# The last pair's token rows moved to the experts and back in pieces of three, sorted by TensorE

## The chip, the cores and the metric

The kernel runs on one core of one Trainium2 chip. The time is device microseconds of one execution. The core has five engines that each run a program of their own and meet through semaphores: PE (TensorE, matrix products), DVE (VectorE), ACT (ScalarE), POOL (GpSimd) and SP (SyncE, which here only issues DMAs).

## What is computed

One layer of a vision transformer on 16 images, 1024 tokens each, 64 channels: patches are embedded, a linear attention with a residual follows, and then a mixture of 16 experts of which every token uses its two best:

```python
logits = einsum('bsd,de->bse', x, gate_w) + gate_b
top_probs, top_idx = top_k(softmax(logits), 2)
top_probs = top_probs / sum(top_probs)
hidden = silu(einsum(x, w1[e])) * einsum(x, w2[e])      # per expert, 64 -> 128
out = h + sum over the token's two experts of top_probs[e] * (hidden @ w3[e])
```

The reference works out all 16 experts for each token. The kernel works out the two that count.

## The kernel before

**Pairs.** The images go through in 8 pairs, m = 0 to 7. A pair has 2048 tokens, which lie on the 128 partitions as 16 columns j. Each token has two expert places r = 0, 1.

**Sorting by expert.** DVE and PE find, for each token and each of its two experts, a row of a scratch tensor in DRAM in which the rows of an expert lie together, each expert padded to whole tiles of 128 rows (`place`). POOL sends the rows there: `scatter(m, j)` (L497) issues, for one column, two indirect DMAs of 128 rows of 512 B (the row of z in two parts, `z_parts`). So a pair has 32 scatters. When they have landed, SP loads the rows back in groups g of four tiles (`load_rows`, L364); a pair has 12 groups, all pairs 96, and g = 84 to 95 are those of pair 7.

**The experts, group by group.** `turn(g)` (PE, L1153) transposes the rows, ACT copies them to SBUF (`rowsT`, L608). `project_in(g)` (PE, L1169) first reads the experts of its four tiles into registers (L1162) and then multiplies with those experts' w1 and w2, in two halves, each as w_hi and w_lo. ACT takes a tanh of each half (`activate`, L618), DVE multiplies (`multiply`, L970 and L972: silu as 0.5 x (1 + tanh(x/2)) times the second product). `turn_hidden` (PE, L1179), `copy_hidT` (ACT, L626), `project_out` (PE, L1186), `copy_y` (ACT, L631) follow, and SP stores y to a second scratch tensor (L373).

**Back to the tokens.** `gather(m, j)` (POOL, L514) issues two indirect DMAs per column that read the token's two result rows of 256 B. For each quarter q of the columns, `weigh` (ACT, L643) multiplies the first by its gate and adds the mean, `sum_up` (DVE, L981, L985) adds the second times its gate and then h, and SP stores the result (L380). For pair 6 the gathered rows lie in the tiles hx and kexp, for the others in `sums`.

**What sets the order.** Every engine runs the same loop over steps s, each with its own list of what belongs to a step, and executes strictly in that order. Group g's `project_in` stands in step s = g + 23. Pair m's attention begins at step BEGUN[m]. The tables SCATTER and GATHER say at which step POOL starts pair m's scatters and gathers, SUMS at which step ACT and DVE weigh and sum quarter q. POOL has 8 x 32 scatters and 8 x 32 gathers, 512 DMAs; for pairs 6 and 7 it does: scatters of pair 7, gathers of pair 5, of pair 6, of pair 7. PE's step is project_in(g), turn_hidden(g - 1), attention, turn(g + 2), project_out(g - 2). ACT's is rowsT of g + 1, copy_y(g - 3), attention, activate(g), copy_hidT(g - 1), weigh. DVE's is attention, multiply(g), attention, sum_up.

Of the kernel before, what the change touches and what calls it, by code (L numbers as in the profile page):

```python
# [18 lines left out]
E = 64  # L19
# [8 lines left out]

GROUP = 4
GROUPS = 12  # L30
TILES = GROUP * GROUPS
assert TILES * P >= 2 * 2 * TOKENS + (EXPERTS - 1) * (P - 1)
SLOTS = TILES * P
# [10 lines left out]
    qturn mixed attend added squares2 ssq2 normed2 zturn zparts logits pick rank odds count base ends owner""")  # L44
# [3 lines left out]
             rank=14, odds=15, count=14, base=14.5, ends=14.5, owner=15)  # L48
# [3 lines left out]
             rank=16, odds=15.5, count=16.5, base=17, ends=17.5, owner=18)  # L52
# [57 lines left out]
def vit_kernel(nc, x, tok_w, tok_b, pos, wk, bk, wq, bq, wv, bv, wr, br, gate_w, gate_b, w1, w2, w3, out):  # L110
    xi_dram = nc.dram_tensor("xi_scratch", (2, 2, TOKENS, E), F32, kind="Internal").ap()
    rows_dram = [nc.dram_tensor(f"rows_scratch{n}", (SLOTS, 2 * E), F32, kind="Internal").ap() for n in range(3)]
    y_dram = [nc.dram_tensor(f"y_scratch{n}", (SLOTS, E), F32, kind="Internal").ap() for n in range(3)]
    with ExitStack() as ctx:
# [14 lines left out]
        before_f = sb("before_f", [P, P])  # L129
        before_b = sb("before_b", [P, P], BF16)  # L130
# [21 lines left out]
        br_in = sb("br_in", [P, E])  # L152
# [68 lines left out]
        tiles_all = sb("tiles_all", [EXPERTS, P])  # L221
# [18 lines left out]
        hidT = [hidT_all[:, n] for n in range(2)]  # L240

# [7 lines left out]
        def rows_of(place):  # L249
# [5 lines left out]
        zeros = tanh  # L255

# [16 lines left out]
            odds_sum_ready gate_ready gates_ready rank_ps_ready tiles_ready tiles_spread base_ps_ready ends_ready  # L273
            past_ready owner_ps_ready owner_ready ranked place_summed place_ready
# [6 lines left out]
        scattered = [sem(f"scattered{n}") for n in range(3)]  # L281
        rows_in = [sem(f"rows_in{n}") for n in range(3)]
# [6 lines left out]
        WEIGHTS = 7 + 6 + 2 + 2 + 10 + 2 + 1 + 2 + 3  # L289
# [33 lines left out]
        def part_of(m, n):  # L323
# [4 lines left out]
            return slice(t0, t1), src[:, 0:(t1 - t0) * 2 * MIXW].rearrange("p (t b e) -> p t b e", b=2, e=MIXW)  # L328

# [5 lines left out]
        def _(sp):  # L335
# [896 lines left out]
```

## Time and profile before

| | |
|---|---|
| median of 3 runs | 793.08 us (792.98 to 795.68) |
| profiled execution, its span | 791.9 us |
| PE busy | 578.2 us, 73% |
| POOL busy | 518.2 us, 65% |
| DVE busy | 441.7 us, 56% |
| ACT busy | 347.6 us, 44% |

The profile is of one execution with a span of 791.9 us, 1.2 us under the median of the timed runs. Busy shares are over the whole span; they do not say which engine is waited for at its end. Times in rows are microseconds from the start of the span, "[32.02 <-DMA ...]" is the idle time of that engine just before the row and what ended it, "issue" is idle time in which the engine waited for nothing that the profile shows. PE's ends are modelled, so its times are read from start to start.

### The profile page before, as it was taken

The page shows a single profiled execution, that of the slowest core. Times are in us where ns is not written, and L with a number is a line of the kernel's source. Part 1 is how long each engine was busy: PE and PEld are TensorE (multiplying, and loading weights), DVE is VectorE, ACT ScalarE, POOL GpSimd, SP SyncE. Part 2 cuts the span into 40 slices and gives each one's busy share as a digit, 9 for nine tenths or more (in the row PEclk, how much of TensorE's full clock was granted, in tenths as well). Part 3 has the DMA queues.
Part 4 walks back from the last instruction along what each step waited for, and adds up shares of the span by engine and source line. Part 5 has one row for each costly group of instructions (what it writes and reads, how often), then busy time and mean ns, then how long its engine had stood idle before and what let it go on. Part 6 is the DMA issues. An engine that isn't in the chain of part 4 may idle for free.

```text
span 791.9 us, 14201 instructions
## 1 busy us (share of the span) xinstructions
PE 578.2 (73%) x3856; PEld 476.0 (60%) x3856; DVE 441.7 (56%) x1237; ACT 347.6 (44%) x753; POOL 518.2 (65%) x540
## 2 busy tenths in 40 slices
PE   5967796787799989998899889998958702883000
PEld 3455545574588678867786678687958702873000
DVE  5664755556447686676667567756765601454111
ACT  2124122152456476647564566446626701674111
POOL 2052246576771777777777777777777777777774
PEclk9976796798999999999999999979979965996555
DMA  2499022333553375528542744374345414544111
GB/s 78 101 229 396 28 71 83 97 97 90 148 170 89 72 188 142 144 53 208 136 124 69 190 130 121 76 175 109 112 117 128 114 51 127 135 100 98 40 40 31
DMA packets 168871, 93.20 MB, mean 118 GB/s; under 512 B 99680, under 2 KB 152928, under 8 KB 168800
## 3 DMA queue, kind: packets, MB, share of 16 engines
q1 hardware_dynamic: 151632, 66.71, 32.1%
q0 software_dynamic: 16384, 25.20, 11.6%
q8 instruction: 39, 0.64, 0.3%
q10 hardware_dynamic: 784, 0.39, 0.2%
q14 instruction: 32, 0.26, 0.1%
HBM read 45.06 MB, written 47.19 MB: 116 GB/s over the span
## 4 chain that ended last, share of the span: by engine, by line
POOL 33%; PE 29%; issue 15%; DVE 13%; DMA 7%; ACT 3%; POOLq 0%; ACTq 0%; DVEq 0%; SPq 0%
POOL rows_scratch L497 15%; POOL sums L514 14%; PE wide_ps L1030 5%; PE h_ps L1169 4%; PE y_ps L1186 3%; DMA hx<-xi_scratch 3%; DMA xi_scratch<-xi 2%; POOL hx L514 2%; POOL kexp L514 2%; PE turn_ps L1153 2%; PE wide_ps L1050 2%; PE wide_ps L1129 1%; PE hidT_ps L1179 1%; PE wide_ps L1036 1%; DVE twice_y L970 1%
## 5 line engine op out<-in xcount | busy, mean ns | idle before, releaser
L497 POOL DMA_INDIRECT rows_scratch<-z_parts,place x256 | 254.9, 996 | 128.4 <-issue 74.7
L514 POOL DMA_INDIRECT sums<-y_scratch,place x224 | 213.8, 955 | 82.7 <-issue 66.4
L1169 PE MATMUL h_ps<-w_hi,rowsT 128*128 x384 | 111.5, 320 | 40.9 <-DVE hid_all L972 33.8
L970 DVE SCALAR_TENSOR_TENSOR twice_y<-tanh,h_ps 128x256 f32<-128x256 f32 x192 | 79.8, 416 | 101.3 <-ACT tanh L618 85.3
L1169 PEld LDWEIGHTS h_ps<-w_hi,rowsT 128*128 128x128 f32 x384 | 74.6, 194 | 55.8 <-issue 54.5
L1186 PE MATMUL y_ps<-w_sb,hidT_all 128*128 x768 | 100.9, 276 | 1.1 <-ACT twice_y L631 1.1
L1169 PE MATMUL h_ps<-w_lo,rowsT 128*128 x384 | 101.0, 290 | 0.0
L1186 PEld LDWEIGHTS y_ps<-w_sb,hidT_all 128*128 128x128 f32 x768 | 97.4, 199 | 2.2 <-issue 2.2
L1153 PE MATMUL turn_ps<-ident,rows_all 128*128 128x128 f32 x384 | 60.8, 282 | 46.3 <-DMA rows_all<-rows_scratch 39.8
L618 ACT ACTIVATE tanh<-h_ps 128x256 f32<-128x256 f32 x192 | 69.8, 387 | 56.3 <-PE h_ps L1169 50.0
L972 DVE SCALAR_TENSOR_TENSOR hid_all<-twice_y,h_ps 128x256 f32<-128x256 f32 x192 | 80.8, 421 | 6.6
L1153 PEld LDWEIGHTS turn_ps<-ident,rows_all 128*128 128x128 f32 x384 | 45.7, 145 | 60.0 <-DMA rows_all<-rows_scratch 40.3
L608 ACT ACTIVATE rowsT<-turn_ps 128x512 fp32r<-128x512 f32 x96 | 57.1, 594 | 44.8 <-PE turn_ps L1153 44.8
L1169 PEld LDWEIGHTS h_ps<-w_lo,rowsT 128*128 128x128 f32 x384 | 75.5, 197 | 0.2
L631 ACT ACTIVATE twice_y<-y_ps 128x256 f32<-128x256 f32 x96 | 36.7, 382 | 63.9 <-DMA y_scratch<-twice_y 51.5
L1179 PE MATMUL hidT_ps<-ident,hid_all 128*128 128x128 f32 x384 | 60.4, 282 | 0.5 <-DVE hid_all L972 0.5
L626 ACT ACTIVATE hidT_all<-hidT_ps 128x512 f32<-128x512 f32 x96 | 57.9, 603 | 5.5 <-PE hidT_ps L1179 2.8
L1030 PE MATMUL wide_ps<-w_patch,x_cols 64*128 64x512 f32 x224 | 57.6, 645 | 3.1 <-DVE w_patch L693 3.1
L981 DVE SCALAR_TENSOR_TENSOR sums<-sums,gate 128x64 f32<-128x64 f32 x112 | 24.5, 280 | 58.3 <-ACT sums L643 56.7
L643 ACT ACTIVATE sums<-sums,mean_all,gate 128x64 f32<-128x64 f32 x112 | 39.9, 430 | 35.8 <-DMA sums<-y_scratch,place 35.8
L1179 PEld LDWEIGHTS hidT_ps<-ident,hid_all 128*128 128x128 f32 x384 | 46.0, 145 | 0.7 <-DVE hid_all L972 0.7
L1030 PEld LDWEIGHTS wide_ps<-w_patch,x_cols 64*128 64x128 f32 x224 | 21.8, 200 | 23.5 <-issue 18.9
(252 smaller groups left out, 910.3 us busy)
## 6 DMA issues: line engine op xcount, KB each, us to landing
rows_all<-rows_scratch SPq DMA_DIRECT2D x96, 256.0 KB
y_scratch<-twice_y SPq DMA_DIRECT2D x96, 128.0 KB
rows_scratch<-tanh SPq DMA_DIRECT2D x3, 3072.0 KB, 19.4
xi_scratch<-xi SPq DMA_DIRECT2D x16, 256.0 KB
rows_scratch<-z_parts,place POOLq DMA_INDIRECT x256
hx<-xi_scratch SPq DMA_DIRECT2D x14, 256.0 KB
sums<-y_scratch,place POOLq DMA_INDIRECT x224
out<-sums SPq DMA_DIRECT2D x56, 64.0 KB
```

The lines of the kernel that those rows point to most:

```text
L497: gp.indirect_dma_start(rows_dram[n], bass.IndirectOffsetOnAxis(ap=place[m % RING][:, r, j:j + 1], axis=0), z_parts[m % 2][:, j // 2, j % ...
L514: gp.indirect_dma_start(y_of[r][apart(m)][:, j // 2, j % 2, :], None, y_dram[m % 3], bass.IndirectOffsetOnAxis(ap=place[m % RING][:, r, j: ...
L608: sc.activation(rowsT[g % 2][:, :], turn_ps[:, :], ACT.Copy).then_inc(S["rowsT_ready"], 1)
L618: sc.activation(tanh[:, j, :], h_ps[:, :].rearrange("p (j n h) -> p j n h", j=GROUP, n=2)[:, j, 0, :], ACT.Tanh, scale=0.5).then_inc(S["ta ...
L626: sc.activation(hidT[g % 2][:, :], hidT_ps[:, :], ACT.Copy).then_inc(S["hidT_ready"], 1)
L970: ve.scalar_tensor_tensor(twice[:, j, :], tanh[:, j, :], 1.0, halves[:, j, 0, :], ALU.add, ALU.mult).then_inc(S["twice_done"], 1)
L972: ve.scalar_tensor_tensor(hid[g % 2][:, j, :], twice[:, j, :], 0.5, halves[:, j, 1, :], ALU.mult, ALU.mult).then_inc(S["hid_done"], 1)
L1030: te.matmul(wide_ps[:, b * 512:(b + 1) * 512], x_cols[second(m)][half, j, :], w_patch[half, j, :, :].rearrange("p t e -> p (t e)"), start= ...
L1153: mm = te.transpose(turn_ps[:, j * P:(j + 1) * P], rows[g % 3][:, j, :, :].rearrange("p n e -> p (n e)"), ident[:, :])
L1169: mm = te.matmul(h_ps[:, j * 256:(j + 1) * 256], rowsT[g % 2][:, j * P:(j + 1) * P], w[:, bass.ds(experts[g][j], 1), :, :].rearrange("d a ...
L1179: mm = te.transpose(hidT_ps[:, j * P:(j + 1) * P], hid[g % 2][:, j, :], ident[:, :])
L1186: mm = te.matmul(y_ps[:, j * E:(j + 1) * E], hidT[g % 2][:, j * P:(j + 1) * P], w3_sb[:, bass.ds(e, 1), :].rearrange("h a d -> h (a d)"), ...
```

## The change

Only pair 7 (`PIECED`) is treated in a new way; registers are read differently for all groups.

- **Pieces.** For each column of pair 7 the 256 rows to be sent are first sorted by expert inside the column and cut into pieces of three neighbouring rows, 96 pieces at most. A piece is sent with one index: 16 DMAs of 96 pieces of 1536 B (`scatter_pieces`) in place of 32 of 128 rows. The tiles of pair 7 hold 126 rows (42 pieces), and pair 7 has 13 groups, g = 84 to 96.
- **Sorting by matrix.** `find_routes` (DVE) makes for each column a 128x288 matrix with a one where a token goes to a slot, `move_rows` (PE) multiplies three 128x96 parts of it with the rows, `take_piece` (ACT) copies the result (96x384) to SBUF. These stand in steps 98 to 102.
- **Gathering pieces.** 16 DMAs of 96 pieces of 768 B (`gather_pieces`). The results are put back by PE: `sum_pieces` multiplies them with one-hot matrices that hold the gates, so that weighing and adding the two experts is one accumulation, and `sum_up_pieces` (DVE) adds h. ACT's weigh and DVE's four instructions of sum_up drop out for pair 7.
- **The gates.** `find_gates(j)` (DVE) makes the 128x288 matrix of gates for column j = s - 108 at the end of its step, `turn_gates` (PE) transposes its three parts at the end of PE's step, `take_gates` (ACT) copies them at the end of ACT's step. These stand in steps 108 to 123.
- **Counting.** For pair 7 the places are worked out from counts per column with a few more matrices, one step more in its plan. POOL makes the constants for this in `sort_consts` (27 instructions) at its start, ahead of splitting the expert weights.
- **Registers.** `load_owners(g + 1)` stands behind the matmuls of project_in(g), and the check of the four values against their bounds is left out.
- **Tables.** GATHER of pair 5 goes from step 104 to 102, of pair 7 from 122 to 123; SUMS of pair 5 from 115-118 to 112-115, of pair 6 from 121-122 to 119-122, of pair 7 from 123-126 to 124-127.

```diff
+PIECE = 3
+PIECES = (2 * P + EXPERTS * (PIECE - 1)) // PIECE
+TILE_PIECES = P // PIECE
+R = TILE_PIECES * PIECE
+PIECED = (7,)
...
+ROUTES = (None, None, None, None, None, None, None, 196)
+GATES = 108
-GATHER = (38, 51, 65, 78, 91, 104, 111, 122)
+GATHER = (38, 51, 65, 78, 91, 102, 111, 123)
...
+            def scatter_pieces(m, j):
+                if j == 0:
+                    wait(pool, "piece_at_ready", 1)
+                    scatter_place(m)
+                wait(pool, "piece_ready", j + 1)
+                gp.indirect_dma_start(pieces_dram[m % 3], bass.IndirectOffsetOnAxis(ap=piece_at[0:PIECES, j:j + 1], axis=0),
+                                      pieces[j][0:PIECES, :], None).then_inc(pieces_out, 16)
...
+            def gather_pieces(m, j):
+                q = j // (COLS // QUARTERS)
+                if j == 0:
+                    for n in range(2):
+                        wait_on(pool, y_stored[n], 16 * ((START[m + 1] + 1 - n) // 2))
...
+                gp.indirect_dma_start(y_pieces[j][0:PIECES, :], None, y_dram[m % 3].rearrange("(c i) e -> c (i e)", i=PIECE),
+                                      bass.IndirectOffsetOnAxis(ap=piece_from[0:PIECES, j:j + 1], axis=0)).then_inc(gathered[0][q], 16)
...
+            def take_gates(j):
+                wait(act, "gates_ps_ready", j + 1)
...
+                sc.activation(pieces[j][0:PIECES, :], piece_place(j)[0:PIECES, 0:PIECE * P], ACT.Copy).then_inc(S["gates_turned"], 1)
...
                 for m, q in sums_at(s):
-                    weigh(m, q)
+                    if m not in PIECED:
+                        weigh(m, q)
+                if 0 <= s - GATES < COLS:
+                    take_gates(s - GATES)
...
+            def find_routes(m, js):
+                for j in js:
...
+                    ve.tensor_scalar(route[i % ROUTE_RING][:, :, :], slot_id[:, :, :], slot[:, 0, j:j + 1], None,
+                                     ALU.is_equal).then_inc(S["route_begun"], 1)
+                for j in js:
...
+                    ve.scalar_tensor_tensor(route[i % ROUTE_RING][:, :, :], slot_id[:, :, :], slot[:, 1, j:j + 1],
+                                            route[i % ROUTE_RING][:, :, :].bitcast(F32), ALU.is_equal, ALU.add).then_inc(S["route_ready"], 1)
+            def find_gates(j):
...
+                wait(dve, "gates_ps_ready", j - 1)
+                wait(dve, "route_gated", 3 * j)
+                there, gated = gated_route[j % 2][:, :, :], gated_route[2][:, :, :]
+                ve.tensor_scalar(there, slot_id[:, :, :], slot[:, 0, j:j + 1], gate[n][0][:, j:j + 1], ALU.is_equal, ALU.mult).then_inc(S["route_gated"], 1)
+                ve.tensor_scalar(gated, slot_id[:, :, :], slot[:, 1, j:j + 1], gate[n][1][:, j:j + 1], ALU.is_equal, ALU.mult).then_inc(S["route_gated"], 1)
+                wait(dve, "route_gated", 3 * j + 2)
+                ve.tensor_tensor(there, there, gated, ALU.add).then_inc(S["route_gated"], 1)
...
                 for m, q in sums_at(s):
-                    sum_up(m, q)
+                    if m in PIECED:
+                        sum_up_pieces(m, q)
+                    else:
+                        sum_up(m, q)
+                if 0 <= s - GATES < COLS:
+                    find_gates(s - GATES)
...
+            def turn_gates(j):
+                wait(pe, "route_gated", 3 * j + 3)
+                wait(pe, "piece_ready", COLS)
+                wait(pe, "gates_turned", j - 1)
+                for n in range(PIECE):
+                    mm = te.transpose(piece_place(j)[0:PIECES, n * P:(n + 1) * P], gated_route[j % 2][:, n, :], ident[:, :])
+                mm.then_inc(S["gates_ps_ready"], 1)
+            def sum_pieces(m, q):
...
+                    for n in range(PIECE):
+                        mm = te.matmul(quarter_place(q)[:, i * E:(i + 1) * E], pieces[j][0:PIECES, n * P:(n + 1) * P],
+                                       y_pieces[j][0:PIECES, n * E:(n + 1) * E], start=(n == 0), stop=(n == PIECE - 1))
...
-                _, experts[g] = nc.values_load_multi_w_load_instructions(owner[m % 3][0:1, i * GROUP:(i + 1) * GROUP], engines=[te.engine],
-                                                                         min_val=0, max_val=EXPERTS - 1)
...
+                if g + 1 < GROUPS_ALL:
+                    load_owners(g + 1)
...
                 for m, k in steps_at(s):
                     attend(m, k + 0.75)
+                if 0 <= s - GATES < COLS:
+                    turn_gates(s - GATES)
+                for m, q in sums_at(s):
+                    if m in PIECED:
+                        sum_pieces(m, q)
```

On POOL, the scatters of pair 7 before, behind the gathers of pair 4 (`sums`, L514) and ahead of those of pair 5:

```order
L514 DMA sums<-y_scratch,place 128x64 x32
L497 DMA rows_scratch<-z_parts,place 6144x128 x32
L514 DMA sums<-y_scratch,place 128x64 x32
L514 DMA hx<-y_scratch,place 128x64
L514 DMA kexp<-y_scratch,place 128x64
```

And now, where the pieces lie in tiles that are free by then (w_patch, x_in, x_cols, squares):

```order
L691 DMA sums<-y_scratch,place 128x64 x32
L661 DMA rows_scratch<-w_patch,piece_at 3744x384 x10
L661 DMA rows_scratch<-x_in,piece_at 3744x384 x2
L661 DMA rows_scratch<-x_cols,piece_at 3744x384 x2
L661 DMA rows_scratch<-squares,piece_at 3744x384 x2
L691 DMA sums<-y_scratch,place 128x64 x32
L691 DMA hx<-y_scratch,place 128x64
L691 DMA kexp<-y_scratch,place 128x64
```

The 32 scatters are 16 DMAs of pieces; the 32 gathers at the end of POOL's program are 16 of L703 in the same way.

On PE, the end of a group's step and the start of the next, before, among the last groups of pair 7 (L1186 is project_out, L1162 the registers, L1169 project_in):

```order
L1186 ISA
L1186 MATMUL y_ps<-w_sb,hidT_all 128x64
L1162 TENSOR_LOAD owner
L1162 ISA x8
L1169 ISA
L1169 MATMUL h_ps<-w_hi,rowsT 128x256
```

And now (L1614 is project_out, L1548 turn_gates, L1593 project_in, L1577 load_owners, L1606 turn_hidden):

```order
L1614 ISA
L1614 MATMUL y_ps<-w_sb,hidT_all 128x64
L1548 MATMUL wide_ps<-ident,gated_route 96x128 x3
L1593 ISA
L1593 MATMUL h_ps<-w_hi,rowsT 126x256
```

The reading of the registers and the 8 rows of the check are gone from ahead of project_in; in their place stand, in steps 108 to 119, three transposes that wait for DVE.

On ACT, one step of the last groups now (L807 rowsT, L833 copy_y, L818 tanh, L827 copy_hidT, L860 weigh, L848 take_gates):

```order
L807 ACTIVATE rowsT<-turn_ps 128x504
L833 ACTIVATE twice_y<-y_ps 126x256
L818 ACTIVATE tanh<-h_ps 126x256 x2
L827 ACTIVATE hidT_all<-hidT_ps 128x504
L860 ACTIVATE sums<-sums,mean_all,gate_0 128x64 x4
L848 ACTIVATE w_patch<-wide_ps 96x384
L807 ACTIVATE rowsT<-turn_ps 128x504
```

Before, the rows of such a step were the same without L848: the copy of the gates now stands between a step's weigh and the next step's rowsT, copy_y and tanh.

## Rows read from the trace of the kernel before

**Rows 1.** The page: the chain that ended last, by line.

```profile
POOL rows_scratch L497 15%; POOL sums L514 14%; PE wide_ps L1030 5%; PE h_ps L1169 4%; PE y_ps L1186 3%; DMA hx<-xi_scratch 3%; DMA xi_scratch<-xi 2%; POOL hx L514 2%; POOL kexp L514 2%; PE turn_ps L1153 2%; PE wide_ps L1050 2%; PE wide_ps L1129 1%; PE hidT_ps L1179 1%; PE wide_ps L1036 1%; DVE twice_y L970 1%
```

**Rows 2.** POOL from 252 us on: gathers (busy us, mean ns | idle before), timeline.

```profile
L514 POOL DMA_INDIRECT sums<-y_scratch,place x224 | 213.8, 955 | 82.7 <-issue 66.4 <-PE turn_ps L1153 15.9 <-DMA y_scratch<-twice_y 0.3
...
252.40 0.98 POOL L514 DMA_INDIRECT sums<-y_scratch,place  x1 [14.73 <-PE turn_ps L1153]
```

**Rows 3.** POOL's timeline (start us, us) at the ends of its last stages.

```profile
622.77 1.03 POOL L497 DMA_INDIRECT rows_scratch<-z_parts,place  x1 [0.30 <-issue]
...
662.01 0.96 POOL L497 DMA_INDIRECT rows_scratch<-z_parts,place  x1 [0.30 <-issue]
...
743.74 0.94 POOL L514 DMA_INDIRECT sums<-y_scratch,place  x1 [0.30 <-issue]
...
782.82 0.94 POOL L514 DMA_INDIRECT sums<-y_scratch,place  x1 [0.30 <-issue]
```

**Rows 4.** Timeline of the end.

```profile
785.18 1.43 ACT L643 ACTIVATE sums<-sums,mean_all,gate 128x64 f32<-128x64 f32 x4 [8.60 <-DMA sums<-y_scratch,place]
...
787.55 0.42 DVE L985 TENSOR_TENSOR sums<-sums,h 128x256 f32<-128x256 f32 x1
```

**Rows 5.** Where pair 7's rows arrive: SP's timeline, and PE's.

```profile
664.27 0.37 SPq L364 DMA_DIRECT2D rows_all<-rows_scratch  x1
...
667.17 1.12 PE L1153 MATMUL turn_ps<-ident,rows_all 128*128 128x128 f32 x4 [32.02 <-DMA rows_all<-rows_scratch]
```

**Rows 6.** PE's timeline in the last groups: first matmul of project_in.

```profile
678.80 0.38 PE L1169 MATMUL h_ps<-w_hi,rowsT 128*128 x1
...
700.26 0.38 PE L1169 MATMUL h_ps<-w_hi,rowsT 128*128 x1 [0.63 <-DVE hid_all L972]
```

**Rows 7.** Weight loads of w_hi from 675 to 720 us, by line.

```profile
L1169 PEld LDWEIGHTS h_ps<-w_hi,rowsT 128*128 128x128 f32 x48 | 9.0, 187 | 8.3 <-issue 8.3
```

**Rows 8.** ACT's and DVE's timelines in a late step with weigh and sum_up.

```profile
704.55 0.87 ACT L618 ACTIVATE tanh<-h_ps 128x256 f32<-128x256 f32 x2 [0.91 <-PE h_ps L1169]
...
707.30 0.58 ACT L608 ACTIVATE rowsT<-turn_ps 128x512 fp32r<-128x512 f32 x1
...
708.18 0.90 ACT L618 ACTIVATE tanh<-h_ps 128x256 f32<-128x256 f32 x2
...
708.68 0.41 DVE L970 SCALAR_TENSOR_TENSOR twice_y<-tanh,h_ps 128x256 f32<-128x256 f32 x1
709.13 0.42 DVE L972 SCALAR_TENSOR_TENSOR hid_all<-twice_y,h_ps 128x256 f32<-128x256 f32 x1
709.46 0.41 DVE L970 SCALAR_TENSOR_TENSOR twice_y<-tanh,h_ps 128x256 f32<-128x256 f32 x1
```

**Rows 9.** DVE, by line: a TENSOR_SCALAR of 128x512.

```profile
L722 DVE TENSOR_SCALAR qv_bias<-ones 128x512 fp32r<-128x512 f32 x1 | 0.4, 361 | 0.0
```

**Rows 10.** Timeline: a TENSOR_SCALAR that starts during a DMA of POOL.

```profile
357.96 0.94 POOL L514 DMA_INDIRECT sums<-y_scratch,place  x1 [0.31 <-issue]
...
358.40 0.54 DVE L934 TENSOR_SCALAR tiles_all<-ones,tiles 16x128 f32<-16x128 f32 x1
```

**Rows 11.** Windows: busy us of each engine, granted clock, DMA share, GB/s.

```profile
57.00:60.00 3.00, 1.88 (x8) 1.48 (x8) 1.01 (x2) 0.29 (x1) 3.00 (x2) 0.66 1.03 382
471.00:474.00 3.00, 1.58 (x12) 1.44 (x12) 2.93 (x8) 2.21 (x8) 2.39 (x3) 1.00 0.72 199
675.00:720.00 45.00, 37.17 (x297) 35.21 (x297) 24.22 (x68) 31.64 (x77) 34.03 (x37) 0.99 0.49 117
```

**Rows 12.** The last y: timeline; and DMA issues with us to landing.

```profile
720.64 1.97 PE L1186 MATMUL y_ps<-w_sb,hidT_all 128*128 x8 [0.67 <-ACT twice_y L631]
...
723.05 0.37 SPq L373 DMA_DIRECT2D y_scratch<-twice_y  x1
...
out<-base SPq DMA_DIRECT2D x8, 64.0 KB, 1.7
```

**Rows 13.** POOL from 0 to 60 us, by line.

```profile
L479 POOL CAST w_hi<-sums 128x1024 fp32r<-128x1024 f32 x4 | 4.1, 1037 | 43.6 <-DMA w_sb<-in_L_ffn_w 43.6
```

More of the change, by code:

```diff
@@ L27 @@
 COLS = 2 * BLOCKS
-GROUP = 4
[L30 to L33, printed above, removed]
+PIECE = 3
[3 more added lines that the diff above has]
+PIECED = (7,)
+GROUP = 4
+GROUPS = tuple(13 if m in PIECED else 12 for m in range(PAIRS))
+START = tuple(sum(GROUPS[:m]) for m in range(PAIRS + 1))
+GROUPS_ALL = START[PAIRS]
+TILES = GROUP * max(GROUPS)
+assert GROUP * min(GROUPS) * P >= 2 * 2 * TOKENS + (EXPERTS - 1) * (P - 1)
+assert PIECES <= P and TILES >= (COLS * PIECES + EXPERTS * (TILE_PIECES - 1)) // TILE_PIECES
+SLOTS = TILES * R
+SPARE = -(-SLOTS // (PIECE * PIECES))
+DRAM_PIECES = (SPARE + COLS) * PIECES
+BOTH = 512
+assert PIECE * PIECES <= BOTH and SLOTS * BOTH < 2 ** 23 and (SPARE + COLS) * PIECE < 256
+ROUTE_RING = 3
 MIXW = E + 1
@@ L97, in apart, with nth, width, pair_of @@
     return int(m == APART)
+def nth(m):
+    return sum(n < m for n in PIECED)
+def width(m):
+    return R if m in PIECED else P
+def pair_of(g):
+    m = max(n for n in range(PAIRS) if START[n] <= g)
+    return m, g - START[m]
 def summed_there(m):
     return -1 if apart(m) else m - 2 if m == PAIRS - 1 else m - 1
-GROUPS_ALL = GROUPS * PAIRS
 HALVES = (slice(0, GROUP // 2), slice(GROUP // 2, GROUP))
@@ L240, in vit_kernel @@
         hidT = [hidT_all[:, n] for n in range(2)]
+        one = PIECE * 2 * E
+        flat = (w_patch[:, :, :, :].rearrange("p j t e -> p (j t e)"), x_in0[:, :, :].rearrange("p r f -> p (r f)"),
+                x_cols0[:, :, :].rearrange("p j c -> p (j c)"), squares[:, :])
+        pieces = [place[:, n * one:(n + 1) * one] for place, count in zip(flat, (10, 2, 2, 2)) for n in range(count)]
+        assert len(pieces) == COLS and one == PIECE * P
         x_in = (x_in0[:, :, :], twice_y[:, :].rearrange("p (r f) -> p r f", r=2))
@@ L304, in sums_at, with routes_at @@
                         yield m, q
+        def routes_at(half):
+            for m in PIECED:
+                for j in range(COLS):
+                    if ROUTES[m] + j // 2 == half:
+                        yield m, j
         def wait(eng, name, count):
@@ L328, in part_of, with wait_scattered, piece_place, quarter_place @@
             return slice(t0, t1), src[:, 0:(t1 - t0) * 2 * MIXW].rearrange("p (t b e) -> p t b e", b=2, e=MIXW)
+        def wait_scattered(eng, m):
+            if m in PIECED:
+                eng.wait_ge(pieces_out, 16 * COLS)
+            else:
+                eng.wait_ge(scattered[m % 3], 16 * 2 * COLS * sum(n % 3 == m % 3 and n not in PIECED for n in range(m + 1)))
+        def piece_place(j):
+            return wide_ps[:, j % 2 * 512:(j % 2 + 1) * 512]
+        def quarter_place(q):
+            return (turn_ps[:, 0:COLS * E // QUARTERS], hidT_ps[:, 0:COLS * E // QUARTERS],
+                    h_ps[:, 0:COLS * E // QUARTERS], h_ps[:, 512:512 + COLS * E // QUARTERS])[q]
         def x_half(m, b, par):
@@ L529, in gathers_at @@
                             yield m, j
+            sort_consts()
             split_experts()
@@ L534, in _ @@
                     wait(pool, "rowsT_ps_ready", min(s - LAG + 2, GROUPS_ALL))
+                for half in (2 * s - 1, 2 * s):
+                    for m, j in routes_at(half):
+                        scatter_pieces(m, j)
                 for m, j in scatters_at(s):
@@ L664, in _ @@
                     copy_hidT(g - 1)
+                for m, j in routes_at(2 * s - 1):
+                    take_piece(m, j)
                 for m, k in steps_at(s):
@@ L1111, in attend @@
+                if k == plan.base and m not in PIECED:
+                    wait(pe, "tiles_spread", m + 1)
+                    te.matmul(slots, tiles_all[0:EXPERTS, :], tiles_to_rows[:, :, :].rearrange("q j e -> q (j e)"), start=False, stop=True)
+                    te.matmul(side_ps[0:EXPERTS, 259:260], upto[:, :], tiles[:, :], start=True, stop=True).then_inc(S["base_ps_ready"], 1)
                 if k == plan.owner:
@@ L1200, in _ @@
                     attend(m, k)
+                for m, j in routes_at(2 * s - 1):
+                    move_rows(m, j)
                 if 0 <= g + 2 < GROUPS_ALL:
```

429 lines of the change are left out of this document (349 added, 80 removed).

## The prediction

> **What bounds the kernel now.** I read the page first. PE has the most busy time, but that is a share over the whole span; the chain that ended last is led by POOL's scatters (L497) and gathers (L514) [rows 1]. So I asked who POOL waits for. From 252.40 us on, its gathers wait for next to nothing: of 82.7 us idle in 224 gathers 66.4 is "issue", the 0.30 between two DMAs, and of the rest one wait of 14.73 ends exactly at 252.40 [rows 2]. Of the 512 DMAs 96, the scatters of pairs 0 to 2, lie before that. The other 416 are a conveyor whose last one starts at 782.82: 530.4 / 415 = 1.28 us each. The reader should see that the rate does not depend on bytes: a scatter writes 512 B per row and took 0.96 at 662.01, a gather reads 256 B and took 0.94 at 782.82 [rows 3].
>
> Then the last part of the conveyor [rows 3]: the scatters of pair 7 from 622.77 to 662.01, the gathers of pairs 5 and 6 up to 743.74, those of pair 7 to 782.82. Behind the last lie its landing, the weighing on ACT, the sum on DVE and the store to the end at 791.9 [rows 4].
>
> PE is the opposite case: it stands still for 32.02 us until pair 7's rows arrive at 667.17 [rows 5], works through the last groups at 3.58 us each (678.80 to 700.26 is six) [rows 6], and the last y goes to its store at 723.05, 20 us before POOL starts to gather from it [rows 3, 12]. This slack of 20 us is where the change puts work.
>
> **The change part by part.**
>
> *POOL.* 32 + 32 DMAs of pair 7 become 16 + 16. From 743.74 to 782.82 are 31 intervals of 1.26 us, so 32 x 1.26 = 40.2 us. The trace has no DMA of 96 pieces of 1536 or 768 B. Bounds: paid by bytes, 0.96 against 0.94 for twice as many adds 0.02 per doubling, up to 1 us in all, and if the longest DMA beside a busy DVE (1.03 at 622.77) became the rule, 3; fewer index rows (96 for 128) could gain as much. I take 1.26. Pair 7's last scatter then starts at 622.77 + 15 x 1.26 = 641.7, and POOL has done pairs 5 and 6 at 642.9 + 80.5 = 723.4.
>
> *Making the pieces* (find_routes, move_rows, take_piece, steps 98 to 102). For 16 columns DVE has 16 x (0.36 + 0.42) = 12.5 us more [rows 8, 9], in order with multiply. Some of it falls into DVE's idle time; I charge 10.5 (0 to 12.5). PE reaches the turn of group 84 at 635.15 now (667.17 less 32.02), so at some 645.7. The rows come when the last scatter has landed: the load was issued 2.26 after that scatter's start (662.01, 664.27) and PE got its rows 2.90 later. With 0.5 more for the larger scatter, an estimate, T0 = 641.7 + 2.8 + 2.9 = 647.3. The making is hidden by the stall; without that cover it would cost the 10.5.
>
> *Registers.* Before each group PE reads four owners and checks them, ahead of the weight load of w_hi, whose idle time is "issue": 8.3 us for 12 groups [rows 7]. That is what this edit can give, 0.7 a group. After 252.40 POOL hides it. Some 16 groups run ahead of it, 11 us at most; part of their time is a wait for loads, so I take 4 (0 to 11). Against it stand 27 POOL instructions of sort_consts. They lie in POOL's idle 43.6 us ahead of w_hi [rows 13], but read beside DVE's first work: no row shows them together, and I take 2 (0 to 5). Net gain at 252.40: 2 us (-5 to +11).
>
> *The gates* (find_gates, turn_gates, take_gates, steps 108 to 123). This decides. DVE makes column j's gates behind multiply(g), PE turns them at the end of the same step, ahead of project_in(g + 1), and ACT copies them at its step's end, ahead of the next tanh. So steps that overlapped become a ring: project_in, tanh, multiply, gates, turn, copy, tanh. Let gates be ready at W. From rows 8, a hand-over between engines is 0.11 (ACT's two tanh start at 708.18 and take 0.90 together, so the first ends some 0.39 in; DVE starts at 708.68).
> - Four turns took 1.12 at the low clock [rows 5], so three at full clock about 0.47; with two hand-overs the copy starts at W + 0.69.
> - rowsT and copy_y hold ACT 0.88 together (707.30 to 708.18), so 0.44 for a copy, and three copies stand ahead of tanh: W + 2.01. DVE's first multiply is at W + 2.51, and its four instructions follow by 0.45, 0.33, 0.45, 0.33: done at W + 4.07.
> - find_gates: a TENSOR_SCALAR of 128x512 took 0.36 [rows 9]; I take 0.35 twice for 128x288 with two pointers, and 0.46 for the sum of 288 columns (256 took 0.42 [rows 4]). Next gates at W + 5.23, with DVE's own hand-over **5.3 us a step** in place of 3.58.
>
> Bounds: 0.25 for each gives 5.1; 0.54 for each, the longest small one [rows 10], 5.7. PE's own work fits in: 37.17 us in 45 for 12 groups, 3.1 each [rows 11].
>
> In steps 112 to 115 and 119, weigh and sum_up of pairs 5 and 6 stand ahead of the gates. From tanh (704.55) to the DVE instruction behind sum_up (708.68) is 4.13, against 2.06 without: 7.4 us. Step 120 has no tanh: 0.69, two copies and hidT's (1.32), weigh to sum_up 2.37 and 0.42 [rows 4], gates 1.16, so 6.0; step 121 has one copy less, 5.5.
>
> Step 108 starts some 10 us after T0 (11.6 before, 667.17 to 678.80, after a long stall; 7.2 for two groups at 3.58), at 657.3. Seven steps of 5.3, five of 7.4 and 6.0 are 80.1: 737.4; step 121 ends at 742.9. The last copy_y is behind the copy of the gates: 0.69 + 0.44 + 0.39, 744.4. The store takes a hand-over, 0.37 and 1.7 [rows 12]: 746.6. POOL, ready at 723.4, waits there **23 us**. The stall moves from PE to POOL.
>
> A rule that speaks against the change: a TENSOR_SCALAR of 16x128 that started 0.44 us into a POOL DMA took 0.54 [rows 10], more than the 0.36 of one of four times as many columns [rows 9]. So some of the 28 TENSOR_SCALARs of the ring will be held by some 0.27 each; at one in four, 2 us, which stand in the range. The Trainium skill, "SBUF — State Buffer", section "Who interferes with whom", says more: DVE in a two-port mode, which tensor_scalar can enter, and GpSimd lock each other out for a whole instruction. By that sentence alone each would wait for the rest of the DMA that runs; the one row agrees that there is a hold, and does not show its full length.
>
> *The clock.* In three us with 1.88 us of PE work the granted clock fell to 0.66, in others with 1.58 it stayed at 1.00 [rows 11]; the ring has some 1.75 of 3 (3.1 in 5.3). At the low level the three turns take some 0.4 more, 14 x 0.4 = 6; more when PE's work, slowed to half, exceeds the ring. I take 2 (0 to 10).
>
> *The end.* 746.7 + 15 x 1.25 = 765.4, landing 2.36 [rows 3, 4]: 767.8. sum_pieces of the last quarter: 12 matmuls of fp32 in two passes, 24 records; eight of y_ps took 1.97 at the low clock [rows 12], so 3.0 to 5.9: 4. DVE's sum starts at 771.9, and as now 4.35 are left (787.55 to 791.9): 776.3.
>
> Sum: 776.3 - 2 + 2 = 776.3 of span. The profiled span of before is 791.9, 1.2 under the median 793.08; with that, **777.5 us**, 2% faster, where POOL alone would have given 5%.
>
> **The rivals.**
> - *POOL stays the bound.* If the ring were hidden, all 40.2 us come out: 791.9 - 40.2 - 2, plus 1.8 for PE's sum in place of weigh and sum_up, plus 1.2: 753. It needs y stored by 723.4, so 14 steps shorter by 1.7 us each. For it: 20 us of slack and no checks on PE. Against: each term of the ring has a row.
> - *A part of it.* A ring of 4.6 (copies that overlap more, a larger register part) gives 14 x 0.7 = 10 less: 767.
> - *The slower side: DVE locked out by POOL.* If a TENSOR_SCALAR waits for the whole DMA that runs, and the next DMA gets in between the two, each waits up to 0.95: 14 x 1.9 = 27, so 804. With the mean rest, 0.36 each (half of 0.95, in 0.95 of 1.26 us), 14 x 0.72 = 10: 787. From 1.4 us a step upward it is slower than before by over 0.5%. For it: 0.54 in rows 10. Against: it started 0.50 before that DMA's end and was held for about half of that. The section of the Trainium skill named above is the rule behind this case.
> - *No change:* 12 us more from clock, locks and a late PE at T0 together give 789.
>
> **How the numbers follow.** A measurement tells about 0.5%, 4 us, from no change: faster is under 789.1, slower over 797. Chances: my forecast (767 to 789) 0.62; POOL as the bound 0.18; between them 0.08; no change 0.06; slower 0.06. The range, which may leave out 2 in 10, goes from POOL's bound, 752, to 789; that of the likeliest case alone is 767 to 787.
>
> **What would show it.** Right: in the waits of POOL one of about 23 us at pair 7's first gather, for a y store; 480 DMAs; from 657 to 740 DVE, PE and ACT idle for each other in turn, project_in every 5.3 and 7.4 us; PE's stall at T0 under 5 us. Wrong: if POOL's idle is still 0.3 everywhere, POOL stayed the bound; if L1277 or L1278 has means over 0.6 us, DVE was locked out; if the DMAs of L661 and L703 are far from 0.95 us, the conveyor does not run by the DMA; if PE has no stall at T0, the pieces were made too late.

## The result and the profile after

The changed kernel takes 780.56 us (median of 4 runs, 778.07 to 784.67) where the kernel before takes 793.15 in the same comparison: a ratio of 0.984, 95% interval 0.981 to 0.987. The forecast was 777.5. The profiled execution has a span of 782.9 us, so it lies at the slow end of the four; before, it was 791.9. Two executions that count as slow, 798.52 us of the registers alone and 765.11 us of both edits again, stand in the medians and ranges below, but not in the ratios.

The waits of POOL behind 260 us (engine, line, released by: us in total, times, longest), POOL's two groups of piece DMAs, and POOL's timeline answer to [rows 2, 3]:

```profile
POOL sums L703 <- DVE base L1317: 24.6, 1, 24.6
```

```profile
L703 POOL DMA_INDIRECT sums<-y_scratch,piece_from x16 | 14.8, 925 | 29.2 <-DVE base L1317 24.6 <-issue 4.6
L661 POOL DMA_INDIRECT rows_scratch<-w_patch,piece_at x10 | 9.9, 992 | 3.0 <-issue 2.1 <-ACT w_patch L842 0.3 <-ACT x_in L842 0.3
```

```profile
256.67 0.99 POOL L691 DMA_INDIRECT sums<-y_scratch,place  x1 [15.73 <-PE turn_ps L1571]
...
627.13 1.16 POOL L661 DMA_INDIRECT rows_scratch<-w_patch,piece_at  x1 [0.30 <-issue]
...
646.21 0.92 POOL L661 DMA_INDIRECT rows_scratch<-squares,piece_at  x1 [0.30 <-issue]
...
752.70 0.96 POOL L703 DMA_INDIRECT sums<-y_scratch,piece_from  x1 [24.63 <-DVE base L1317]
...
771.17 0.92 POOL L703 DMA_INDIRECT sums<-y_scratch,piece_from  x1 [0.31 <-issue]
```

POOL issues 32 DMAs fewer: the 16 scatters of pieces start 1.27 us apart on average, the 16 gathers 1.23. In exchange it stands still for 24.63 us in front of pair 7's results. The name behind the wait is a guess by time: by its code this gather waits for sums of pair 5, long done, and for the stores of y. PE's stall, and SP's last store of y:

```profile
651.87 0.75 PE L1571 MATMUL turn_ps<-ident,rows_all 126*128 126x126 f32 x4 [3.76 <-DMA rows_all<-rows_scratch]
...
749.86 0.34 SPq L478 DMA_DIRECT2D y_scratch<-twice_y  x1
```

The gather starts 2.84 us behind the issue of that store; in the three runs below that have such a wait too, it is 2.84 to 2.85. PE's wait for pair 7's rows, 32.02 us in [rows 5], is 3.76 us now. The stall moved from PE to POOL, as forecast.

Why the last y is so late is seen in one step, in the timeline of PE, ACT and DVE (weight loads, POOL and SP left out):

```profile
676.57 0.42 DVE L1277 TENSOR_SCALAR gated_route<-slot_id,slots_f,gate 128x288 f32<-128x288 f32 x1
...
677.37 0.46 DVE L1280 TENSOR_TENSOR gated_route<-gated_route 128x288 f32<-128x288 f32 x1
677.88 0.53 PE L1548 MATMUL wide_ps<-ident,gated_route 128*96 128x128 f32 x3 [0.52 <-DVE gated_route L1280]
...
678.45 0.49 ACT L848 ACTIVATE w_patch<-wide_ps 96x384 f32<-96x384 f32 x1 [1.92 <-PE wide_ps L1548]
...
678.84 0.58 ACT L807 ACTIVATE rowsT<-turn_ps 128x504 fp32r<-128x504 f32 x1
...
679.31 0.38 ACT L833 ACTIVATE twice_y<-y_ps 126x256 f32<-126x256 f32 x1
...
679.57 0.66 ACT L818 ACTIVATE tanh<-h_ps 126x256 f32<-126x256 f32 x2
...
680.05 0.42 DVE L1298 SCALAR_TENSOR_TENSOR twice_y<-tanh,h_ps 126x256 f32<-126x256 f32 x1 [2.22 <-ACT tanh L818]
...
681.63 0.42 DVE L1277 TENSOR_SCALAR gated_route<-slot_id,slots_f,gate 128x288 f32<-128x288 f32 x1
681.97 0.56 DVE L1278 TENSOR_SCALAR gated_route<-slot_id,slots_f,gate 128x288 f32<-128x288 f32 x1
682.56 0.46 DVE L1280 TENSOR_TENSOR gated_route<-gated_route 128x288 f32<-128x288 f32 x1
683.08 0.87 PE L1548 MATMUL wide_ps<-ident,gated_route 128*96 128x128 f32 x3 [1.69 <-DVE gated_route L1280]
```

Read it as a ring: turn 677.88, copy 678.45, rowsT, copy_y, tanh 679.57, multiply 680.05, gates 681.63 to 683.02, turn 683.08. It takes 5.20 us, and each engine stands idle in it for another: PE 1.69 us ahead of the turn, ACT 1.92 ahead of the copy, DVE 2.22 ahead of its multiply. The tanh follows copy_y without a wait, so here the way leads over ACT's three copies and not over project_in. The 16 turns start 5.06, 5.27, 5.20, then (with sums of pair 5) 8.10, 7.96, 7.24, 7.54, then 5.41, 5.06, 5.06, and (with sums of pair 6) 6.88, 6.25, 5.58, 5.59 us apart; the last two are 1.37.

The end answers to [rows 4]: PE's sums (L1562) and DVE's last:

```profile
774.57 2.77 PE L1562 MATMUL h_ps<-sums,x_cols 96*128 96x64 f32 x12
...
777.13 2.77 PE L1562 MATMUL h_ps<-sums,squares 96*128 96x64 f32 x12
...
779.93 0.42 DVE L1307 TENSOR_TENSOR sums<-h_ps,h 128x256 f32<-128x256 f32 x1 [4.70 <-PE h_ps L1562]
```

### The profile page after: what moved, and what is told of

Its sections match the earlier page's. It is cut to its first block, busy times and chain, and to the rows that moved or that the text cites. A ratio compares the mean times of both kernels' runs of the same rounds, so it can differ in the third digit from the quotient of the medians.

```text
span 782.9 us, 13961 instructions
## 1 busy us (share of the span) xinstructions
PE 640.1 (82%) x4059; PEld 534.8 (68%) x4059; DVE 477.1 (61%) x1322; ACT 353.7 (45%) x774; POOL 503.8 (64%) x537
## 4 chain that ended last, share of the span: by engine, by line
PE 50%; DVE 25%; issue 9%; ACT 7%; DMA 5%; POOL 3%; ACTq 0%; SPq 0%; DVEq 0%; POOLq 0%
PE h_ps L1593 7%; PE wide_ps L1381 7%; PE y_ps L1614 5%; PE hidT_ps L1606 4%; DVE twice_y L1298 3%; PE turn_ps L1571 3%; PE wide_ps L1401 2%; PE wide_ps L1504 2%; POOL rows_scratch L674 2%; ACT sums L860 2%; PE wide_ps L1387 2%; DMA hx<-xi_scratch 2%; PE wide_ps L1449 1%; DMA xi_scratch<-xi 1%; PE wide_ps L1450 1%
## 5 line engine op out<-in xcount | busy, mean ns | idle before, releaser
L1298 DVE SCALAR_TENSOR_TENSOR twice_y<-tanh,h_ps 128x256 f32<-128x256 f32 (+1 forms) x194 | 80.5, 415 | 83.1 <-ACT tanh L818 65.1
L1593 PE MATMUL h_ps<-w_hi,rowsT 128*128 (+1 forms) x388 | 121.2, 337 | 12.1 <-DVE hid_all L1300 12.1
L1593 PE MATMUL h_ps<-w_lo,rowsT 128*128 (+1 forms) x388 | 109.3, 305 | 0.0
L1614 PE MATMUL y_ps<-w_sb,hidT_all 128*128 (+1 forms) x776 | 107.3, 286 | 1.8 <-ACT twice_y L833 1.8
L1614 PEld LDWEIGHTS y_ps<-w_sb,hidT_all 128*128 128x128 f32 (+1 forms) x776 | 104.4, 209 | 3.5 <-issue 3.4
L1593 PEld LDWEIGHTS h_ps<-w_hi,rowsT 128*128 128x128 f32 (+1 forms) x388 | 81.9, 211 | 20.8 <-issue 17.4
L818 ACT ACTIVATE tanh<-h_ps 128x256 f32<-128x256 f32 (+1 forms) x194 | 69.4, 387 | 40.3 <-PE h_ps L1593 36.0
L1300 DVE SCALAR_TENSOR_TENSOR hid_all<-twice_y,h_ps 128x256 f32<-128x256 f32 (+1 forms) x194 | 81.6, 421 | 6.6
L1593 PEld LDWEIGHTS h_ps<-w_lo,rowsT 128*128 128x128 f32 (+1 forms) x388 | 82.7, 213 | 0.3
L807 ACT ACTIVATE rowsT<-turn_ps 128x512 fp32r<-128x512 f32 (+1 forms) x97 | 57.5, 593 | 39.7 <-PE turn_ps L1571 39.7
L1606 PE MATMUL hidT_ps<-ident,hid_all 128*128 128x128 f32 (+1 forms) x388 | 69.0, 308 | 6.9 <-issue 3.2
L827 ACT ACTIVATE hidT_all<-hidT_ps 128x512 f32<-128x512 f32 (+1 forms) x97 | 58.6, 604 | 17.2 <-PE hidT_ps L1606 16.0
L1606 PEld LDWEIGHTS hidT_ps<-ident,hid_all 128*128 128x128 f32 (+1 forms) x388 | 50.8, 158 | 12.3 <-issue 10.3
L833 ACT ACTIVATE twice_y<-y_ps 128x256 f32<-128x256 f32 (+1 forms) x97 | 37.0, 381 | 31.7 <-DMA y_scratch<-twice_y 22.6
L1548 PE MATMUL wide_ps<-ident,gated_route 128*96 128x128 f32 x48 | 11.5, 364 | 33.2 <-DVE gated_route L1280 33.2
```

Of the source, the lines that this page charges most:

```text
L807: sc.activation(rowsT[g % 2][:, 0:GROUP * w], turn_ps[:, 0:GROUP * w], ACT.Copy).then_inc(S["rowsT_ready"], 1)
L818: sc.activation(tanh[0:w, j, :], h_ps[0:w, :].rearrange("p (j n h) -> p j n h", j=GROUP, n=2)[:, j, 0, :], ACT.Tanh, scale=0.5).then_inc(S ...
L827: sc.activation(hidT[g % 2][:, 0:GROUP * w], hidT_ps[:, 0:GROUP * w], ACT.Copy).then_inc(S["hidT_ready"], 1)
L1298: ve.scalar_tensor_tensor(twice[0:w, j, :], tanh[0:w, j, :], 1.0, halves[:, j, 0, :], ALU.add, ALU.mult).then_inc(S["twice_done"], 1)
L1300: ve.scalar_tensor_tensor(hid[g % 2][0:w, j, :], twice[0:w, j, :], 0.5, halves[:, j, 1, :], ALU.mult, ALU.mult).then_inc(S["hid_done"], 1)
L1593: mm = te.matmul(h_ps[0:w, j * 256:(j + 1) * 256], rowsT[g % 2][:, j * w:(j + 1) * w], w12[:, bass.ds(experts[g][j], 1), :, :].rearrange(" ...
```

## The experiments

**Gates a step later.** PE turns and ACT copies the gates that DVE made in the step before; the same work.

```diff
-                if 0 <= s - GATES < COLS:
-                    turn_gates(s - GATES)
+                if 0 <= s - GATES - 1 < COLS:
+                    turn_gates(s - GATES - 1)
```

(and the same with take_gates on ACT)

> The changed kernel with one edit: PE turns and ACT copies the gates of a column one step after DVE has made them; the work is the same. Theory (a ring DVE, PE, ACT, DVE is closed in each step because PE and ACT wait for gates of the same step): the steps fall from 5.1 to 8.1 us to about 4 to 5, the last y is stored before POOL has finished pair 6, POOL's wait of 24.6 us falls under 5 and the time to 756 to 760. Rival (steps are long since TENSOR_SCALAR is held beside POOL's DMAs and PE runs at the low clock): steps stay above 5 us, 775 or more. Rival (the gates' work itself is what fills DVE and ACT): some 770.

Measured 761.36 us (760.52 to 761.86; ratio to before 0.957, 0.954 to 0.961), 1.4 us above the expected 756 to 760 and well under both rivals. The turns of PE, POOL at the first gather of pieces, and ACT in a late step:

```profile
666.40 0.49 PE L1548 MATMUL wide_ps<-ident,gated_route 128*96 128x128 f32 x3
...
670.41 0.49 PE L1548 MATMUL wide_ps<-ident,gated_route 128*96 128x128 f32 x3
```

```profile
728.11 0.93 POOL L703 DMA_INDIRECT sums<-y_scratch,piece_from  x1 [0.30 <-issue]
```

```profile
719.21 1.43 ACT L860 ACTIVATE xi<-hx,mean_all,gate 128x64 f32<-128x64 f32 x4 [8.04 <-DMA kexp<-y_scratch,place]
```

Up to 706 us the turns are 2.8 to 4.3 us apart, and POOL has no long wait behind 256.30: the ring was the cause of the whole wait. The last turns are 6.9 to 10.2 us apart, since there ACT waits for POOL's gathers of pair 6: POOL is the bound. The work of the gates is the same and fills no engine.

**Constants later.** POOL makes the sorting constants behind split_experts().

```diff
-            sort_consts()
             split_experts()
+            sort_consts()
```

> The changed kernel with one edit: POOL makes the sorting constants after it has split the expert weights, not before. Theory (the constants' reads and writes run beside DVE's set-up from 31 to 42 us and hold it, which starts POOL's unbroken run at 256.7 instead of 252.4): the maximum of the keys on DVE is back at some 39 us (38.3 in the kernel before, 43.1 in the changed one), the long wait of POOL ends near 252, and the time falls by 4 us to about 776. Rival (the front is late because of the extra instructions on DVE and PE themselves, not because of POOL beside them): POOL's wait still ends at 256 or later, 780.

Measured 784.49 us (783.11 to 785.75; 0.986, 0.983 to 0.990): no gain, and above both expectations. In the timeline of DVE and PE the place does what it should. The changed kernel, then this one:

```profile
35.73 1.31 DVE L986 TENSOR_SCALAR turn_cols<-ident,turn_cols 128x64 f32<-128x64 f32 x2
...
37.49 1.75 DVE L989 TENSOR_TENSOR qv_bias<-qs 1x512 fp32r<-1x512 f32 x1
39.30 3.78 PE L1504 MATMUL wide_ps<-hx,proj_k 128*128 128x512 f32 x4 [4.19 <-DVE qv_bias L989]
43.11 1.23 DVE L1042 TENSOR_REDUCE kmax<-wide_ps 128x1 f32<-128x1024 f32 x1 [3.87 <-PE wide_ps L1504]
```

```profile
35.27 0.42 DVE L986 TENSOR_SCALAR turn_cols<-ident,turn_cols 128x64 f32<-128x64 f32 x2
...
36.17 0.68 DVE L989 TENSOR_TENSOR qv_bias<-qs 1x512 fp32r<-1x512 f32 x1
36.91 1.98 PE L1504 MATMUL wide_ps<-hx,proj_k 128*128 128x512 f32 x4 [1.75 <-DVE qv_bias L989]
38.93 1.22 DVE L1042 TENSOR_REDUCE kmax<-wide_ps 128x1 f32<-128x1024 f32 x1 [2.08 <-PE wide_ps L1504]
```

Beside POOL's constants a pair of TENSOR_SCALARs took 1.31 us for 0.42 and a TENSOR_TENSOR 1.75 for 0.68, and the maximum of the keys came 4.2 us later. Only 2.4 of these are DVE's: PE's four products start that much later. The other 1.8 are PE's own, 3.78 us for 1.98, at a granted clock of 0.50 (1.2 GHz) from 39 to 43 us against 1.00 (2.4 GHz) from 36.8 to 39. But POOL's unbroken run started at 259.23 here, against 256.67: the 4.2 us were gone again by then.

**Both edits.** The two diffs above together.

> Both edits together: constants after the split, gates turned and copied a step later. If POOL is then the bound from its first unbroken DMA on, the two gains add up to the whole of POOL's saving: 752 to 755, with no wait of POOL over 5 us behind some 252 us. If the front's loss were hidden behind another wait, it is no better than the gates' edit alone (756 to 760).

Measured 758.78 us (757.16 to 759.4; 0.955, 0.951 to 0.958). POOL started at 251.48 and had no long wait behind that, as the theory said, but the time lies in the rival's range. The end grew: the last gather starts at 742.18 and DVE's last sum at 752.42, 10.2 us later, where it was 4.7 in [rows 3, 4]. It is 10.2 with the gates a step later alone, too.

**The changed kernel again,** with no edit.

> The changed kernel itself, beside the others on this chip, since its four runs spread from 778.1 to 784.7 while single kernels of the same chip agreed within 2 us. If the spread is that of the start of POOL's unbroken run (256.7 in the profile, 251.5 to 259.2 in its variants), this profile has POOL's start and its span displaced by about the same amount against the first: 778 to 785.

Measured 780.24 us (778.73 to 783.76; 0.981, 0.975 to 0.986). POOL's start is 257.85, its wait 22.1 us, the span 782.0. Span and median agree with the first ones to 1 us, so the place of the constants alone, at 784.49, shows no gain against either.

**The two variants with the open ring again,** side by side on one chip.

> The kernel with gates turned a step later, beside the next one on one chip, since what the place of the constants is worth is smaller than the spread of POOL's start in single profiles (251.5 to 259.2). In this pair POOL is the bound from its start on, so an earlier start shows in full. 759 to 762.

> The kernel with both edits. If the 4 us that DVE's maximum of the keys comes earlier without POOL beside its set-up (38.9 against 43.1) reach POOL's start, it is 4 us under its neighbour; if what follows at either clock level takes most of it back, 0 to 2 us under.

Measured 760.19 (757.3 to 760.9) and 758.38 us (750.78 to 765.11), ratios 0.957 (0.954 to 0.960) and 0.953 (0.949 to 0.957). 1.8 us, with intervals that overlap: it is not settled that the place of the constants gains anything. What goes with POOL's start is the granted clock. Windows of 40 to 250 us, in the order constants later, the changed kernel again, both edits (last three columns: clock, DMA share, GB/s):

```profile
40.00:250.00 210.00, 160.91 (x891) 124.80 (x890) 121.26 (x309) 67.43 (x126) 124.97 (x133) 0.82 0.46 138
```

```profile
40.00:250.00 210.00, 168.03 (x914) 129.89 (x913) 118.67 (x312) 67.83 (x126) 110.75 (x107) 0.81 0.47 138
```

```profile
40.00:250.00 210.00, 165.83 (x950) 130.29 (x951) 123.12 (x319) 71.39 (x132) 125.31 (x133) 0.84 0.47 140
```

POOL starts at 259.23, 257.85 and 251.48 in these. Two more executions with a mean clock of 0.85 start at 252.4 and 252.3, one of them the kernel before. In all twelve profiles POOL starts at 255.5 to 259.2 where this clock is 0.81 or 0.82, and at 251.5 to 254.4 where it is 0.83 to 0.85. With the constants first the six starts are 252.3 to 258.3, with them later the four are 251.5 to 259.2. So the start goes with the clock over a range of some 7 us, more than the gain in question. What tips the clock in one execution or the other stays open, and that the clock is the cause of the late start is not shown.

**Checks back.** The changed kernel with its registers read and checked at the start of project_in; the edit brings back both the place of the reading and the check.

```diff
-                if g + 1 < GROUPS_ALL:
-                    load_owners(g + 1)
...
             def project_in(g):
+                load_owners(g)
...
-                                                                         min_val=0, max_val=EXPERTS - 1,
-                                                                         skip_runtime_bounds_check_because="a count of experts, held to EXPERTS - 1 by find_owners")
+                                                                         min_val=0, max_val=EXPERTS - 1)
```

> The changed kernel with its registers as before: the four owners are read at the start of project_in and checked against their bounds. By the prediction's register term (4 us before POOL's unbroken run starts, hidden behind it) 784; in the ring the reading stands on the path between the turned gates and project_in, but tanh waits for ACT there, so little there. If the register part brings nothing in this kernel (from 158 to 252 us the two traces differ by 0.5): 780 to 782.

Measured 797.06 us (794.27 to 803.44; 1.004, 1.001 to 1.006), 16 us over the changed kernel and no faster than before. Both expectations missed: the price is in the ring. POOL's wait (the profile is of the slowest of the ten runs), and PE's step between the turned gates and project_in (L1592 here):

```profile
POOL sums L703 <- DVE base L1317: 33.4, 1, 33.4
```

```profile
678.72 0.52 PE L1548 MATMUL wide_ps<-ident,gated_route 128*96 128x128 f32 x3
680.13 0.38 PE L1592 MATMUL h_ps<-w_hi,rowsT 128*126 x1 [0.88 <-issue]
```

It is 1.41 us from the turn to project_in, where it is 0.29 without (677.88 to 678.17); in the other steps it is 1.7 to 1.8 against 0.29 to 0.53. The reading stands behind the turn in PE's program, so it adds 1.1 to 1.5 us to each round of the ring that has a project_in. The steps with a project_in become 5.6 to 6.9 us, and 9.2 to 9.3 with sums.

**The registers alone, in the kernel before.** load_owners as in the change, applied to the kernel before.

```diff
             def project_in(g):
-                m, i = divmod(g, GROUPS)
-                wait(pe, "owner_ready", m + 1)
                 if g == 0:
+                    load_owners(0)
...
-                _, experts[g] = nc.values_load_multi_w_load_instructions(owner[m % 3][0:1, i * GROUP:(i + 1) * GROUP], engines=[te.engine],
-                                                                         min_val=0, max_val=EXPERTS - 1)
...
+                if g + 1 < GROUPS_ALL:
+                    load_owners(g + 1)
```

> The kernel before with the registers' part of the change alone: owners of group g + 1 read behind project_in(g), no check. By the prediction only the groups ahead of POOL's unbroken run count: start at 248 instead of 252.4, 789. Rival (nothing, as from 158 to 252 us the kernel before and the changed one take 93.6 and 94.1): 792 to 795. It cannot give 16 us, the price of the checks inside the changed kernel, since POOL is the bound here.

Measured 790.93 us (786.5 to 798.52; 0.996, 0.992 to 1.000): some 3 us, with an interval that begins at nothing; 4 was the forecast. POOL's start and its last gather:

```profile
251.96 0.97 POOL L514 DMA_INDIRECT sums<-y_scratch,place  x1 [15.07 <-PE turn_ps L1153]
...
780.16 0.94 POOL L514 DMA_INDIRECT sums<-y_scratch,place  x1 [0.30 <-issue]
```

The start is 0.4 us earlier than 252.40, not 4, and the last gather 2.7 earlier than 782.82 [rows 2, 3]. So the forecast's way, an earlier start of POOL, is not what this profile shows.

**Gates a step later, with the checks.** The diff of the gates and that of the checks, together.

> Gates turned and copied a step later, and in addition the registers read and checked as in the kernel before. Theory (the check costs 16 us only because it stands on the ring, between the turned gates and project_in): with the ring open POOL has slack of its own again, and the time is 761 to 765 with POOL's wait under 4 us. Rival (the check is a price of the last groups with or without the ring, 1 to 2 us for each of 14 steps): 775 or more.

Measured 759.51 us (756.29 to 761.57; 0.955, 0.949 to 0.961), as without them. With the ring open, POOL is the bound and the checks cost nothing that shows, though the steps are up to 4.5 us. So the 16 us of reading and checking belong to the ring.

**The end.** Both edits, gates begun two steps earlier and ahead of weigh and sum_up, and PE's sum waiting column by column.

```diff
-GATES = 108
+GATES = 106
...
-                wait_on(pe, gathered[0][q], 16 * 2 * COLS // QUARTERS * (gathers(m) - 1) + 16 * COLS // QUARTERS)
                 for i in range(COLS // QUARTERS):
                     j = q * COLS // QUARTERS + i
+                    wait_on(pe, piece_in[j], (16 * 2 * COLS // QUARTERS * (gathers(m) - 1) if i == 0 else 0) + 16)
```

> Constants later and gates a step later, and in addition: gates begin two steps earlier and stand ahead of weigh and sum_up in their step, and PE's sum of the pieces waits for each column instead of each quarter. Theory (in the version with both edits PE's sums at the low clock, 5.1 us a quarter, end 13 us behind the last gather where 9 were spent before): PE starts 4 us earlier on the first column and ends within about 2 us of the last landing, so 4 to 5 us less, 753 to 755. Rival (the last quarter's landing decides): no change.

Measured 755.68 us (753.98 to 758.76; 0.951, 0.945 to 0.957), the fastest here. PE's first sum, DVE's last:

```profile
729.98 2.27 PE L1563 MATMUL turn_ps<-sums,w_patch 96*128 96x64 f32 x8 [16.44 <-DMA sums<-y_scratch,piece_from]
```

```profile
751.32 0.42 DVE L1308 TENSOR_TENSOR sums<-h_ps,h 128x256 f32<-128x256 f32 x1 [4.70 <-PE h_ps L1563]
```

The last gather starts at 745.79: 5.5 us to DVE's last sum in place of 10.2 to 10.3 in the five other profiles with an open ring. The profile shows 4.7 us, as expected; the medians differ by 3.1 from the first run of both edits, and their ranges overlap, so in the time the gain is not settled. Which of the parts of this edit brings it was not tried.

## Why the prediction was right, step by step

- **POOL as a conveyor** held. 64 DMAs became 32, the pieces at 1.27 and 1.23 us from start to start. The price is per DMA: 96 x 1536 B in a scatter took 0.91 to 0.94 us in 12 of 16 DMAs, no more than the 0.96 of 128 x 512 B before. The term of 40.2 us was right.
- **The pieces** are hidden, as forecast: PE still stalled, 3.76 us, for the rows; the forecast was 1.6. The 5.6 us from the last scatter's start to these rows, with 0.5 that no row had shown, were 5.66.
- **The ring** was the deciding step, and it was sized well: 5.06 to 5.41 us against 5.3, 7.2 to 8.1 and 6.9 against 7.4, then 6.25 and 5.58 against 6.0 and 5.5. The experiments with gates a step later show that it was the cause, not only a fit. Inside it find_gates takes 1.26 us (676.57 to 677.83), or 1.39 where an instruction is held (681.63 to 683.02), in place of 1.16, and the way from the finished gates to tanh is shorter (677.83 to 679.57 is 1.74, where 2.01 was forecast); these cancelled, which is luck.
- **POOL's wait** was 24.6 against 23 us and ended at 752.70 against 746.7. Of these 6 us 4.4 were there when the first piece was scattered (627.13 against 622.77). That is the mis-sized term: the **net gain at POOL's start**, forecast as 2 us (-5 to +11), was a loss of 4.3 in this profile (256.67 against 252.40) and of 5.5 in the second. Neither of its parts shows at that start. The registers alone moved the start by 0.4 us, not 4. The constants held DVE's set-up for 2.4 us, near the 2 forecast, but moving them did not bring the start forward. The start goes with the clock from 40 to 250 us, over up to 7 us; why stays open.
- **The locks.** Of the 32 TENSOR_SCALARs of find_gates 16 start while a DMA of POOL runs. Two of these took 0.56 and 0.57, all others 0.41 to 0.43, beside POOL or not; in the second profile of the kernel five of 17 took 0.56 to 0.63. All seven start 0.43 to 0.51 us before the end of a DMA, as the one in [rows 10] did (0.50), and in these two profiles none that starts earlier or later in a DMA was held. The DMA beside the one of 681.97:

```profile
681.45 0.95 POOL L691 DMA_INDIRECT sums<-y_scratch,place  x1 [0.30 <-issue]
```

  So the slower rival is out: none waits for a whole DMA. The rule of the Trainium skill ("SBUF — State Buffer", section "Who interferes with whom") does not describe this: beside DMAs of 0.95 us such an instruction was held by 0.21 at most. For POOL's own elementwise instructions the trace agrees with that section: the TENSOR_TENSOR's 0.68 became 1.75 beside one of 1.19 at 37.50.
- **The clock** in the ring, in windows of 680 to 720 and 720 to 752 us (third column from the right):

```profile
680.00:720.00 40.00, 26.75 (x155) 25.81 (x153) 21.87 (x62) 18.45 (x49) 30.35 (x32) 0.74 0.35 82
720.00:752.00 32.00, 17.09 (x98) 14.56 (x97) 15.18 (x46) 14.64 (x40) 6.24 (x7) 0.67 0.20 45
```

  It was 0.74 and 0.67, so the doubt was justified; the turns took 0.87 for 0.53 in steps at the low level, 0.3 each, and the steps still came out within 0.7 of the forecast.
- **The end** was 2.3 us longer up to DVE's sum (771.17 to 779.93 is 8.8 against 6.5). The 4 us for the last quarter's sum are 5.1, and PE, at 5.1 a quarter, falls behind gathers of 4.9. The store behind it took 3.0, not 4.35, so that by luck more than half of the miss cancels.

In sum it is 782.9 against 776.3 of span, in the slowest of the four runs; the median is 3 us over the forecast. The rival in which POOL stays the bound gave 753, and both edits with the end shortened reach 755.7: it was nearly the right price of another kernel.

## What to carry to other kernels

Work that is put into the idle time of three engines is not free when it is handed on between them inside one step: it turns overlapped steps into a ring, whose length is the sum of its parts, and each small thing on it (reading and checking four registers, 1.1 to 1.5 us) counts once per step. Let the consumer take what the producer made a step ago. When the last engine's share has been halved, look at what comes behind it: here PE's sum was next, 10.2 us behind the last gather's start in place of 4.7.

## What the runs showed of the hardware

PE's sums in the end never got the high clock, though PE had no idle time from 762 to 777 us. Windows of the changed kernel:

```profile
762.00:767.00 5.00, 5.00 (x25) 5.00 (x25) 0.42 (x1) 0.00 (x0) 3.78 (x5) 0.50 0.35 88
767.00:772.00 5.00, 5.00 (x25) 5.00 (x25) 0.42 (x1) 0.00 (x0) 3.78 (x5) 0.50 0.29 74
```

The level was 1.2 GHz (0.50) from 757 to 777 us, and a quarter's 24 products (12 matmuls, recorded twice each) took 5.1 us. The forecast had taken the middle between the two levels. Whether another form of these sums would run at the high level was not tried.

An indirect DMA on POOL took 0.91 to 0.94 us for 96 rows of 768 or 1536 B in 26 of 32 DMAs, against 0.94 to 0.96 for 128 rows of 256 or 512 B in most of the others.
